# Causal attention heads on one Trainium2 core: ten second-sum slots for sixteen, diagonal masks of two units together, parts stored as they are made

## The reference, cut to what matters

```
q, k, v = heads(Wq, bq), heads(Wk, bk), heads(Wv, bv)     # 16 heads, 2048 x 8 each
q, k = rope(q), rope(k)
att = q k^T / sqrt(8);  att = where(key <= query, att, -1e10)
y = softmax(att) v;  out = y Wp^T + bp
```

## Time and profile before

| | |
|---|---|
| median of 3 runs | 5308.29 us (5307.76 to 5311.03) |
| the profiled execution's own time | 5303.91 us |
| its span | 5302.1 us |
| busy: PE, DVE, ACT, POOL | 4591.2 (87%), 3222.8 (61%), 2658.1 (50%), 995.7 (19%) us |
| mean granted clock of TensorE | 0.912 of 2.4 GHz |
| causal stage, first maxima to last multiply | 368.5 to 983.6 us of the span |
| PE's turn of head 15's maxima (L976) in the causal stage | 934.3 us |
| plain, local, filtered stage, first maxima | 2548.3, 3423.1, 4289.5 us |

### The profile page before, as it was taken

The page is one execution under the profiler, slowest core; times in us unless marked ns, Lnnn a source line. Parts: engine busy times, 40 slices in busy tenths (PEclk is TensorE's granted clock), DMA queues, the critical chain, the costliest instruction groups (busy, mean ns, idle before and its releaser), DMA issues. The chain is left out here.

```text
span 5302.1 us, 66018 instructions
## 1 busy us (share of the span) xinstructions
PE 4591.2 (87%) x22489; PEld 1703.4 (32%) x22489; DVE 3222.8 (61%) x4626; ACT 2658.1 (50%) x4904; POOL 995.7 (19%) x957
## 2 busy tenths in 40 slices
PE   6979999797079999857899997688879969999899
PEld 3432222343033333224222222355544412222244
DVE  4355555334865555245888884435973388888433
ACT  2325555333323434423488886334433348888633
POOL 0000000000017878810000000035960000000000
PEclk8979999898589999967799998788989979999999
DMA  1021000000000000000200000120000020000000
GB/s 61 20 62 38 30 28 26 14 16 4 0 8 3 5 3 6 5 28 0 67 26 25 25 25 2 40 70 9 1 1 20 14 59 27 30 28 25 3 20 20
DMA packets 46687, 118.42 MB, mean 22 GB/s; under 512 B 17162, under 2 KB 18186, under 8 KB 45354
## 3 DMA queue, kind: packets, MB, share of 16 engines
q1 hardware_dynamic: 38065, 96.18, 6.0%
q10 hardware_dynamic: 4320, 15.73, 0.8%
q0 software_dynamic: 4000, 2.67, 0.4%
HBM read 81.99 MB, written 19.01 MB: 19 GB/s over the span
## 5 line engine op out<-in xcount | busy, mean ns | idle before, releaser
L1087 DVE TENSOR_REDUCE 66_heads_mx<-66_heads_mps 128x1 f32<-128x1024 f32 x512 | 602.4, 1218 | 65.7 <-PE 66_heads_mps L965 64.5
L1087 DVE TENSOR_REDUCE 41_heads_mx<-41_heads_mps 128x1 f32<-128x1024 f32 x512 | 602.2, 1218 | 65.1 <-PE 41_heads_mps L965 63.9
L1061 ACT ACTIVATE 41_heads_p<-41_heads_sps 128x512 f32<-128x512 f32 x1024 | 552.8, 596 | 112.6 <-PE 41_heads_sps L986 109.0
L1061 ACT ACTIVATE 66_heads_p<-66_heads_sps 128x512 f32<-128x512 f32 x1024 | 552.8, 596 | 112.0 <-PE 66_heads_sps L986 108.5
L1087 DVE TENSOR_REDUCE 9_heads_mx<-9_heads_mps 128x1 f32<-128x1024 f32 (+7 forms) x384 | 332.8, 908 | 229.3 <-PE 9_heads_mps L968 223.3
L1993 ACT ACTIVATE 27_latent_heads_p<-27_latent_heads_ring 128x512 f32<-128x512 f32 x512 | 277.3, 594 | 385.4 <-PE 27_latent_heads_ring L1912 373.1
L2011 DVE TENSOR_REDUCE 27_latent_heads_mx<-27_latent_heads_ring 128x1 f32<-128x512 f32 x512 | 322.9, 684 | 197.7 <-PE 27_latent_heads_ring L1892 197.7
L1061 ACT ACTIVATE 9_heads_p<-9_heads_sps 128x512 f32<-128x512 f32 (+3 forms) x640 | 314.0, 532 | 232.4 <-PE 9_heads_sps L989 125.7
L986 PE MATMUL 41_heads_sps<-38_head_rows_qs,38_head_rows_ks 123*128 123x512 bf16 x1024 | 311.4, 386 | 4.9 <-ACT 41_heads_p L1061 4.9
L986 PE MATMUL 66_heads_sps<-61_head_rows_qs,61_head_rows_ks 123*128 123x512 bf16 x1024 | 311.3, 386 | 4.9 <-ACT 66_heads_p L1061 4.9
L1868 POOL TENSOR_TENSOR 27_latent_heads_psum<-27_latent_heads_psum,27_latent_heads_p 128x1024 f32<-128x1024 f32 x112 | 263.8, 2355 | 87.7 <-ACT 27_latent_heads_p L1993 87.7
(11 more groups left out here) (1116 smaller groups left out, 7342.1 us busy)
## 6 DMA issues: line engine op xcount, KB each, us to landing
4_experts_wbuf<-in_L0f_experts SPq DMA_DIRECT2D x8, 514.0 KB, 3.5
12_experts_wbuf<-in_L0f_experts SPq DMA_DIRECT2D x8, 514.0 KB, 3.4
60_experts_wbuf<-in_L3f_experts SPq DMA_DIRECT2D x8, 514.0 KB, 3.5
69_experts_wbuf<-in_L3f_experts SPq DMA_DIRECT2D x8, 514.0 KB, 3.4
46_hale_masks_qs<-scratch_q_parts SPq DMA_DIRECT2D x39, 96.0 KB
46_hale_masks_ks<-scratch_k_parts SPq DMA_DIRECT2D x39, 96.0 KB
5_head_rows_qs<-scratch_q_parts SPq DMA_DIRECT2D x28, 96.0 KB
5_head_rows_ks<-scratch_k_parts SPq DMA_DIRECT2D x28, 96.0 KB
```

Source lines behind the costliest of these rows:

```text
L1061: act.activation(pslot[x % PS][:, 0:CW - off], sps[e % SB][:, 0:CW - off], ACT.Exp, scale=SCALE / 2).then_inc(ex_done, 1)
L1087: dve.tensor_reduce(mx[h % 2][:, i, half:half + 1], mps[x % 2][:, 0:w], AX.X, ALU.max).then_inc(mx_taken, 1)
```

## The change

1. *Causal groups.* `exp_steps` makes ten groups of four instead of sixteen of four to one. Key tiles 12 to 15 for chunk 3 stand in the groups of tiles 4 to 7, and tiles 9 and 11 in those of 8 and 10, in the strips of chunks 0 and 1 that are free there ("place" 4 and 5). They must not add to chunks 0 and 1, so they use v from a new tile `Vz`, where 16 columns of zeros stand before the 9 of v: 25 output rows, of which the last 9 are a second accumulator. The four sums of tile 0 clear all 25 rows. SP moves the extra rows to `more` and `z2` (four more DMAs a head), and DVE adds them at the end. POOL fills `Vz` at the start of the stage.
2. *Masks of two units together.* In the causal stage a burst of two units issues the 48-row matmuls of both, then the one or two masks; DVE is told of both units at once.
3. *Parts stored as they are made.* ACT issues each part's stores inside `prepare_heads`. Only head 0 is copied from SBUF, only its lower 48 rows (in the local stage its 72), keys too on SP's queue; the upper rows of head 0 and all of head 1 come from DRAM. Head 0's maxima use the lower rows alone. ACT puts head 0's maxima into the rows.
4. *Smaller parts.* The bias of v is four matmuls of 512 columns ahead of the sixteen instead of one after each. The constant rows of the keys are filled a stage earlier, with runs of 256 elements for 64. The experts' logits stand in `yT`.

```diff
 def exp_steps(causal):
-    for j in range(NT):
-        for c in range(j // TPC if causal else 0, NC):
+    if causal:
+        which = [[(j, c, c) for c in range(NC)] for j in range(4)]
+        which += [[(4 + i, 1, 1), (4 + i, 2, 2), (4 + i, 3, 3), (12 + i, 3, 4)] for i in range(4)]
+        which += [[(8 + i, 2, 2), (8 + i, 3, 3), (9 + i, 2, 5), (9 + i, 3, 4)] for i in (0, 2)]
...
-                def max_unit(x):
+                def max_pass(xs):
+                    for x in xs:
...
+                            low = HIGH if b and h else 0
...
+                    for x in xs:
+                        _i, _half, w, diag = units[x % U]
+                        if diag:
+                            ins = pe.matmul(mps[x % 2][:, w - P:w], g.ident_bf[:], g.mask_q[:], start=False, stop=True)
+                    ins.then_inc(mx_ready, len(xs))
...
+                        if causal and (s == 0 or place >= NC):
+                            at = (SECOND.index(j) * HEADS + h) * (SECOND_AT + ROW) + (SECOND_AT if s == 0 else 0)
+                            ins = pe.matmul(ops[row:row + SECOND_AT + ROW, off:CW], v_flat[:, at:at + SECOND_AT + ROW], p, start=(s == 0),
+                                            stop=True, tile_position=(0, row), skip_group_check=True)
...
                             while x < due(h, n):
-                                max_unit(x)
-                                x += 1
+                                both = causal and x + 1 < due(h, n) and units[x % U][3]
+                                max_pass([x, x + 1] if both else [x])
+                                x += 2 if both else 1
...
                 sp.wait_ge(rows.filled, rows.FILLED)
-                rows.copy_small(sp, 0, m_in[0])
-                for h in range(1, COPIED):
...
+                sp.wait_ge(rows.stored, rows.STORED)
+                load_rows(sp, 1)
+                for a in range(3):
+                    load_queries(g, sp, 0, a, qs[0], m_in[0], (1,))
+                    load_keys(g, sp, 0, a, ks[0], m_in[0], (1,))
+                load_products(sp, 0)
+                load_products(sp, 1)
...
                 pe.wait_ge(weights, 16)
+                for c in range(NC if bv is not None else 0):
+                    pe.matmul(vps[c][:].rearrange("p (t d) -> p t d", d=D), g.W["ones_row"], bv[0:1, :].unsqueeze(1).to_broadcast([1, TPC, D]),
+                              start=True, stop=False, skip_group_check=True)
                 for i in range(NT):
-                    if bv is not None:
-                        ins = pe.matmul(vps[i // TPC][:, tile(i % TPC)], g.W["ones_row"], bv[0:1, :], start=False, stop=True)
```

More of the change, by code:

```diff
@@ L648, in exp_steps @@
 def exp_steps(causal):
+    if causal:
+        which = [[(j, c, c) for c in range(NC)] for j in range(4)]
+        which += [[(4 + i, 1, 1), (4 + i, 2, 2), (4 + i, 3, 3), (12 + i, 3, 4)] for i in range(4)]
+        which += [[(8 + i, 2, 2), (8 + i, 3, 3), (9 + i, 2, 5), (9 + i, 3, 4)] for i in (0, 2)]
+    else:
+        which = [[(j, c, c) for c in range(NC)] for j in range(NT)]
     groups, n = [], 0
-    for j in range(NT):
+    for tiles in which:
         group = []
-        for c in range(j // TPC if causal else 0, NC):
-            group.append((n, c, P * (j % TPC) if causal and c == j // TPC else 0))
+        for j, c, place in tiles:
+            group.append((n, j, c, P * (j % TPC) if causal and c == j // TPC else 0, place))
             n += 1
@@ L691, in __init__ @@
         six = ((0, 0, 0, 1, 1, 2), (0, 1, 2, 0, 1, 0))
-        self.places = [[(low + DH * i, a) for low in (0, HIGH) for i, a in enumerate(six[x])] if doubled else
-                       [(DH * i, (i // 3, i % 3)[x]) for i in range(PAIRS)] for x in range(2)]
+        self.places = six if doubled else [[(i // 3, i % 3)[x] for i in range(PAIRS)] for x in range(2)]
     def fill_keys(self, eng):
@@ L838, in head_loop @@
     groups, S = exp_steps(causal)
+    NG = len(groups)
+    SECOND = [0] + [j for group in groups for _n, j, _c, _off, place in group if place == 4]
+    SECOND_AT = 2 * DH
     units = max_units(causal)
@@ L867, in head_loop @@
         z = st.sb("z", [P, T // A])
+        z2 = st.sb("z2", [P, T // A])
+        more = g.yT[:, 0:T // 2]
+        Vz = st.sb("Vz", [P, len(SECOND) * HEADS + 1 if causal else 1, SECOND_AT + ROW])
+        v_flat = Vz[:].rearrange("p n r -> p (n r)")
         spread = st.sb("spread", [P, A, P])
@@ L878, in head_loop @@
              "o_copied", "spread_in", "inverted", "spread_done", "joined"))
-        STORED = 2 * NC * 16
+        STORED = (2 * NC + (4 if causal else 0)) * 16
         def entry(h, n):
@@ L909, in store @@
                 def store(sp, h):
+                    if causal and h == 0:
+                        sp.wait_ge(dve_cleared, 4)
                     sp.wait_ge(o_copied, h + 1)
@@ L914, in store @@
                         sp.dma_start(z[h * A + 2 * c:h * A + 2 * c + 2, :], osb[h % 2][at + DH:at + ROW, :]).then_inc(o_out[h % 2], 16)
+                    for place, c in enumerate((3, 2) if causal else ()):
+                        at = 32 * place + SECOND_AT
+                        sp.dma_start(more[h * DH:(h + 1) * DH, chunk(c - 2)], osb[h % 2][at:at + DH, :]).then_inc(o_out[h % 2], 16)
+                        sp.dma_start(z2[h * A + 2 * c:h * A + 2 * c + 2, :], osb[h % 2][at + DH:at + ROW, :]).then_inc(o_out[h % 2], 16)
                 def put_maxima(sp, h):
@@ L1092, in _ @@
                     dve.wait_ge(o_out[i], STORED * HEADS // 2)
+                if causal:
+                    dve.tensor_tensor(z[:], z[:], z2[:], ALU.add).then_inc(z_joined, 1)
+                    dve.wait_ge(z_joined, 1)
                 dve.reciprocal(z[:], z[:]).then_inc(inverted, 1)
+                if causal:
+                    dve.tensor_tensor(attnT[:, T // 2:], attnT[:, T // 2:], more, ALU.add).then_inc(z_joined, 1)
+                    dve.wait_ge(z_joined, 2)
                 for c in range(NC):
```

211 lines of the change are left out of this document (104 added, 107 removed).

## The result

| | before | the change |
|---|---|---|
| median of the runs | 5308.02 us (4 runs) | 5233.40 us (4 runs, 5228.28 to 5238.46) |
| span of the profiled execution | 5302.1 | 5226.5 us |
| ratio to before | | 0.9859 (95% interval 0.9842 to 0.9876) |

What follows compares the result with a forecast made beforehand. PE was taken to set the causal heads' period. Loop -55.6, rest of the causal stage -14.2, plain -7.2, filtered -3.8, local -6 sum to -86.8: from 5308.3 to 5221 us, range 5165 to 5265 (forecast's own 5200 to 5240).

Steps and rivals of the forecast that it cites:

- The period: Causal loop, time per head between ACT's copy-outs: from 35.95 to 32.5 us, a gain of 3.45.
- Masks together, -2.57: Causal heads: two changes of PE's kind fewer in each of 12 bursts, 0.107 each, saving 2.57 us a head.
- Sums, -5.15: Causal heads: ten groups for sixteen, -4.5, and six changes of kind fewer, -0.64; 5.15 us less PE work a head.
- New waits, 5.3: Causal heads: walking twelve bursts gave PE 5.3 us of waits a head for 1.08, on DVE, ACT, turn and copy-out.
- Head 1's rows, -7.2: Causal stage's start: PE's wait of 7.21 us for rows before head 1's first maxima goes, -7.2.
- lower half alone, +1: Head 0's maxima from the lower half can't overlap halves: +1 us in the causal stage, 0 in the plain one.
- The first head up to its turn, -2.8: Causal loop's first head, up to its turn: 2.8 us shorter, part of the loop's -55.6.
- Preparation: Stage starts before the first maxima, with ACT last instead of PE: causal -8, plain -7.2, filtered -3.8 us.
- Local heads, -6: Local stage: head 1's wait of 11.55 us for key rows, half gained as copies and stores share engines: -6.
- Rival C: Causal sums: 25-row matmuls don't overlap other strips, 0.86 more for each of six groups; about 5268 us, chance 0.08.
- Rival E: Stage starts: stores collide with head 0's copies, heads start 10 us later in each of four stages; 5261 us, chance 0.10.
- B: Causal loop: waits absorbed, only 2.3 us a head left, period 29.5; about 5176 us, chance 0.17.

Runs made afterwards that it cites:

- e3: The change with maxima 8 units ahead for 7 and DVE told of a burst's unmasked unit at once: 5210.0 us, 0.9818 of the kernel before.
- e5: The change with maxima 8 units ahead for 7, DVE still told of both units behind the mask: 5222.9 us (1 run).
- e4: The change, but SP issues head 2's loads only when head 0's row of maxima has landed: 5226.4 us (1 run).
- e1: The change, but each unit is followed by its own mask and DVE is told of each unit: 5217.1 us, 0.9834 of the kernel before.
- e9: e3 plus head 2's loads behind head 0's maxima, copy-out after exponential 5 for 6, and bursts at new places: 5166.0 us, 0.9733.

## Why the prediction was right, and where it was wrong

The time lay in the range and 12 us above the forecast; the forecast's own range (5200 to 5240) holds it. Point by point:

- **The period** came out at 32.68 for 32.5, but by two errors that cancel. *Masks together, -2.57*: the run without them shows 1.43, and 1.63 beside sixteen groups. One reason can be read in the timeline: where a burst stands straight ahead of a group, the change of kind behind the mask stays (515.23 to 515.39). That is so in four of the twelve bursts, 0.43 by the price of 0.107, out of 1.14. The rest of the gap is open. *Sums, -5.15*: 4.3 to 4.5. *New waits, 5.3*: 3.66 (the waits that the prediction lists add up to 5.46, not 5.3). Its mechanism was right and e3 against e5 shows it. The walk through twelve bursts overrated each kind: 2.61 on DVE for 3.76, 0.25 on ACT for 0.7, 0.55 at the turn for 0.7, 0.24 on the copy-out for 0.3. It named waits "in few places" as a sign of being wrong. The 2.61 stand in five of the twelve bursts of a head, which is the number of bursts that its walk had found late, and not the twelve that its list of signs says.
- What I didn't draw from it: by my own numbers (2.57 saved against 4.2 of new waits) the joined masks had to lose on their own. Only the sum of both parts was looked at, and so the prediction didn't say that one part of the change slows the kernel.
- **Head 1's rows, -7.2**: the wait did go, but the stage's start didn't get shorter by it (+1.5). The steps that failed are *lower half alone, +1*, which was 4.0 (a round of one buffer is PE's time plus DVE's, not the longer of the two), and the row of maxima, which I had costed at nothing where it moved to ACT's queue: 4.2 late behind head 2's loads, which e4 takes back. Together -7.2 + 4.0 + 4.2 = +1.0 of the +1.5.
- **The first head up to its turn, -2.8**, was +1.8. The prediction gives no working for it; 33/40 of the loop's 3.45, for the 33 of 40 scores, would be 2.85. The step that failed is that share: a head of the loop has 16 groups of sums before and 10 after, but the first head has only its own sums so far, and up to its turn these are 8 groups before and 7 after. That saves 1.08 by the prediction's prices, where 33/40 of 5.15 is 4.2. e1 bears it out: at the granted clock of before it took 26.29 for this piece, 0.9 less than the 27.21. The second step is that I had priced all of this head at full clock. The windows of the 12 us from the first score on, in the kernel before, e1, the change and e4, show the granted clock at 0.85, 0.85, 0.72 and 0.50:

```profile
403.90:415.90 12.00, 11.31 (x61) 3.03 (x61) 7.61 (x9) 7.74 (x16) 0.00 (x0) 0.85 0.20 72
```

```profile
397.30:409.30 12.00, 11.26 (x61) 3.07 (x61) 6.74 (x8) 7.66 (x16) 0.00 (x0) 0.85 0.09 38
```

```profile
397.00:409.00 12.00, 10.57 (x50) 2.52 (x50) 5.33 (x6) 6.53 (x14) 0.00 (x0) 0.72 0.09 38
```

```profile
393.30:405.30 12.00, 11.11 (x42) 2.42 (x44) 6.46 (x8) 6.10 (x12) 0.00 (x0) 0.50 0.18 67
```

  0.13 of 12 us is 1.6 of work. With the 3.2 that the sums fall short this makes 4.8, about the missing 4.6. (PE's waits on DVE in the piece rose from 1.0 to 2.8 us, but the forecast had such waits in it.) The clock also tells why e4 gave 3.2 and not 4.8: its first score came sooner, but the head then took 30.3 to its first turn (393.27 to 423.60), the first 12 at half clock.
- **Preparation**: causal -8.1 for -8 (25.75 to 17.61; the prediction had 25.3 to 17.3); plain -6.4 for -7.2, and then +1.7 for the 0 of its head 0 (the same round of one buffer, 2.35 for DVE's 2.27); filtered -2.9 for -3.8, then +1.7.
- **Local heads, -6**: -13.0. The contention was as I put it (1.4 to 1.7 a copy for 1.3) and cost 5.0; the step that failed is what it was set against: the copies of head 2, and the wait of 6.62 for them, I had not counted. The kernel before already showed the contention beside its own stores: three key copies held SP's queue for 5.34 us from 3426.45 on, for 1.96 by themselves. How much of the -13.0 will return in another execution is not sure, by the spread of this stage above.
- **The last head and the tail**: -6.1 for -7.4, +2.9 for +2.9. The exact hit of the tail is luck: the piece took 18.2 to 19.7 in the change and the eleven runs, which is +2.8 to +4.3.
- So the total of -74.6 for -86.8 came near by errors that partly cancel: the stage's start and first head gave 12 too little, the local heads 7 more than forecast.
- Rival C fell (0.99 a group). Rival E was in part true (the row of maxima, the local copies), and paid for by head 2's rows. B did not come about in the change, and needs other places and signals: e9 goes past it.
